# A four-layer graph network, software-pipelined over 64 samples: the order of steps on each engine chosen anew

## What is computed

```python
# layer 0: three projections, scores = (x W1)(x W2)^T
e = where(adj, leaky_relu(h1 @ h2.T), -big); out = relu(softmax(e) @ h3)
# layer 1: graph attention
h = x @ W; e = leaky_relu((h @ a1)[:, None] + (h @ a2)[None, :])
out = elu(softmax(where(adj, e, -big)) @ h)
# layer 2: mlp1 (256 to 512), attention without a mask on 512 features, mlp2 (512 to 256), attention with the mask
o = relu(x @ mlp1 + b1);  o = elu(gat(o, None, W_fc, a_fc)) + o
o = relu(o @ mlp2 + b2);  out = relu(elu(gat(o, adj, W_hand, a_hand)) + o)
# layer 3: attention of 4 heads with q, k, v, output projections and biases
out = softmax(mask(q @ k.T / 8)) @ v @ wo.T + bo
```

## Time and profile before

| | |
|---|---|
| three executions | 2769.3, 2783.66, 2788.16 us |
| span of the profiled execution | 2787.8 us |
| granted TensorE clock, mean over the span | 0.974 of full |
| PE busy | 2604.3 us, 93% of the span |
| DVE, ACT, POOL busy | 83%, 71%, 70% |

### The profile page before, as it was taken

How to read it: one execution, slowest core, us unless ns; L and a number is a source line. 1 busy time by engine, 2 the same in 40 slices (tenths; PEclk the granted TensorE clock), 3 DMA queues, 4 the chain that set the end, 5 groups by cost and what they waited for, 6 DMA issues and landing times.

```text
span 2787.8 us, 64765 instructions
## 1 busy us (share of the span) xinstructions
PE 2604.3 (93%) x21448; PEld 2453.2 (88%) x21448; DVE 2308.8 (83%) x6124; ACT 1985.1 (71%) x4801; POOL 1959.6 (70%) x2439
## 2 busy tenths in 40 slices
PE   4789999999999999999999999999999999999864
PEld 4689999999999999999999999999999999998763
DVE  2468888888888988888898898888889888888764
ACT  2357777777777777777777777777777777777642
POOL 1447777777777777777777787778777777776642
PEclk7799999999999999999999999999999999999986
DMA  3123434343443434344443434444343444333332
GB/s 129 49 59 116 136 116 135 116 134 113 126 130 118 133 114 137 112 124 131 123 128 118 131 116 129 123 130 121 118 136 116 127 120 132 120 118 118 95 95 87
DMA packets 317114, 329.67 MB, mean 118 GB/s; under 512 B 35312, under 2 KB 248688, under 8 KB 316784
## 3 DMA queue, kind: packets, MB, share of 16 engines
q1 hardware_dynamic: 316784, 325.54, 38.4%
HBM read 174.41 MB, written 150.99 MB: 117 GB/s over the span
## 4 chain that ended last, share of the span: by engine, by line
PE 34%; DVE 29%; POOL 13%; issue 10%; ACT 7%; DMA 5%; SPq 1%; POOLq 0%; DVEq 0%; ACTq 0%
PE ps L287 22%; POOL xn L1149 6%; DVE att L998 4%; PE ps L526 4%; DMA x0Tp<-in_xT 4%; DVE p L1102 3%; DVE att L993 3%; PE ps L297 3%; DVE p L1087 3%; POOL act L1159 3%; DVE ex L989 2%; DVE act L936 2%; ACT act L605 2%; POOL rstd L1144 2%; PE ps L303 2%
## 5 line engine op out<-in xcount | busy, mean ns | idle before, releaser
L1212 POOL TENSOR_TENSOR p<-p,rd 128x512 f32<-128x512 f32 x256 | 271.8, 1062 | 20.1
L1137 POOL TENSOR_TENSOR x0Tp_lo<-x0Tp,x0Tp_hi 128x512 fp32r<-128x512 f32 x64 | 82.6, 1291 | 288.0 <-ACT x0Tp_hi L542 288.0
L773 ACT ACTIVATE p<-p,nmx 128x256 f32<-128x256 f32 x512 | 256.0, 508 | 12.2 <-DVE nmx L1087 12.2
L1149 POOL TENSOR_SCALAR xn<-act,nmean,rstd 128x256 f32<-128x256 f32 x384 | 237.8, 629 | 23.6 <-POOL rstd L1144 22.5
L287 PE MATMUL ps<-h_lo,proT_hi 128*128 128x256 f32 x512 | 161.0, 314 | 62.9 <-POOL proT_lo L1137 61.9
L1087 DVE CUSTOM_DVE_ANT_0 p<-ps,mask 128x256 f32<-128x256 f32 x512 | 189.3, 417 | 31.2 <-PE ps L500 30.5
L542 ACT ACTIVATE h_hi<-ps 128x512 fp32r<-128x512 f32 x192 | 114.5, 596 | 123.2 <-PE ps L287 123.2
L1137 POOL TENSOR_TENSOR proT_lo<-sco,proT_hi 128x512 fp32r<-128x512 f32 x128 | 166.2, 1299 | 49.4 <-ACT proT_hi L542 49.3
L555 ACT ACTIVATE sco<-sco,nmax 128x256 f32<-128x256 f32 x384 | 190.8, 502 | 7.2 <-DVE nmax L859 6.5
L1159 POOL TENSOR_TENSOR act<-act,x 128x512 f32<-128x512 f32 x64 | 82.9, 1296 | 151.8 <-ACT act L605 151.8
L865 DVE STREAM_TRANSPOSE act<-sco 128x512 f32<-128x512 f32 x192 | 133.2, 694 | 57.2 <-ACT sco L555 56.3
(11 more groups left out here) (239 smaller groups left out, 12805.2 us busy)
## 6 DMA issues: line engine op xcount, KB each, us to landing
scratch<-p SPq DMA_DIRECT2D x128, 512.0 KB, 2.9
p4T<-scratch SPq DMA_DIRECT2D x512, 128.0 KB, 3.4
scratch_pro<-act SPq DMA_DIRECT2D x192, 256.0 KB, 2.4
sco<-scratch_pro SPq DMA_DIRECT2D x768, 64.0 KB, 2.4
x0Tp<-in_xT SPq DMA_DIRECT2D x64, 256.0 KB, 4.4
x<-in_x SPq DMA_DIRECT2D x64, 256.0 KB, 3.1
scratch_o<-sco SPq DMA_DIRECT2D x64, 256.0 KB, 2.0
o3r<-scratch_o SPq DMA_DIRECT2D x256, 64.0 KB, 2.1
```

Source lines behind the costliest of these rows:

```text
L773: ins = nc.scalar.activation(rows_, rows_, ACT.Exp, scale=-1.0, bias=nmx4[:, h, m:m + 1], accum_out=den4[:, h, m:m + 1])
L1137: return G.tensor_tensor(lo, whole, hi.bitcast(fp32), ALU.subtract)
L1149: ins = G.tensor_scalar(xn[:, m, :], y[:, m, :], nmean[i][:, m:m + 1], rstd[i][:, m:m + 1], ALU.add, ALU.mult)
L1212: G.tensor_tensor(rows_, rows_, rd4[:, h, :].unsqueeze(2).unsqueeze(3).broadcast_to([P, NT, QUADS, CT * QP]), ALU.mult).then_inc(S["p4n"], 1)
```

## The change

The five lists are replaced. The steps, their instructions, waits and buffers are the same. Most of the differences in the digits are a shift of a whole list or another place for the round's start, and change nothing. What is left, as moves within the cyclic sequence (all else keeps its place):

- PE: v4 goes ahead of x0; f2 goes from behind a4 to ahead of s0.
- ACT: t3 goes ahead of k2; r2 ahead of h0 and u1; p0 from behind f2 to behind q4; l0 ahead of k4; t1 ahead of b2; n2 ahead of x0; t0 from behind n2 to behind a1, so that o2 and the heads' exponentials come before it; p42 ahead of a1.
- DVE: i0 and i3 go behind s43; p42 goes from behind b1 to ahead of i2; a1 ahead of n2; g0 ahead of x42; r2 ahead of h0 and z3; f2 ahead of ag0, and both ahead of e1; o3 ahead of x1; t1 ahead of a4; x3 ahead of e0; h3 behind st4; t0 behind q4; e3 ahead of d2; ag4 ahead of t3; i1 between s40 and s41.
- POOL: n4 goes behind n3; k4 behind l0; v4 and m2 ahead of d40; t0 from ahead of d40 to between d42 and p42; t3 ahead of d43.
- SP: lt goes ahead of st, o1, o5, lx and o0; o0 goes behind i1 and o3; i3 and o40 ahead of i5.

```diff
 ORDERS = {
-    "sp": "o42:8 i40:8 i42:8 st:9 o1:3 o5:6 lx:1 o0:1 lt:0 i1:3 i0:1 o3:6 i5:6 i3:6 o40:7",
-    "pe": "x0:4 v4:9 b2:7 n2:6 s40:9 v2:7 w2:7 s42:9 a1:5 h1:4 g0:2 c2:6 a0:3 a3:8 f1:4 r2:6 h0:2 m3:7 s0:2 x1:5 a4:9 f2:6 x3:8 m2:5 y4:9 h3:7 q4:8 k4:8 f3:7 d2:6",
-    "ac": "t3:7 c2:5 g0:1 z2:6 a3:7 b3:7 a0:2 h0:1 u1:3 r2:5 m3:6 o3:6 s0:1 x1:4 p1:3 a4:8 x3:7 f2:5 p0:1 w2:5 h3:6 x2:5 m2:4 q4:7 u3:6 k4:7 l0:0 p3:6 b2:5 t1:3 x0:2 n2:4 t0:1 p40:7 o2:4 p41:7 y2:5 a1:3 p42:7 h1:2 p43:7 k2:5",
-    "dv": "i0:2 v2:6 s42:8 p41:8 s43:8 i2:6 b1:4 p42:8 n2:6 h1:3 p43:8 x40:8 a1:4 j2:6 c2:5 x42:8 g0:1 c3:7 z2:6 b3:7 a3:7 st1:4 r3:7 ag1:4 h0:1 z3:7 e1:3 st3:7 ag3:7 st0:2 r2:5 ag0:2 x1:4 a4:8 f2:5 e0:1 x3:7 t1:3 b2:5 y4:8 o3:6 t0:1 h3:6 st4:8 q4:7 d2:5 e3:6 k4:7 v4:7 t3:6 s40:7 s41:7 ag4:8 i3:6 x0:2 p40:7 i1:3",
-    "po": "l0:1 t1:4 t0:2 d40:8 p40:8 m2:5 d41:8 p41:8 d42:8 p42:8 d43:8 p43:8 t3:7 v4:9 y1:4 a0:2 n4:9 v1:4 n1:4 v3:7 n3:7 m3:6 v0:2 k4:7 n0:2 w2:5",
+    "sp": "o42:8 i40:8 i42:8 lt:0 st:9 o1:3 o5:6 lx:1 i1:3 o3:6 o0:1 i0:1 i3:6 o40:7 i5:6",
+    "pe": "f3:6 d2:5 v4:7 x0:2 b2:5 n2:4 s40:7 v2:5 w2:5 s42:7 a1:3 h1:2 c2:4 g0:0 a0:1 a3:6 f1:2 r2:4 h0:0 m3:5 f2:4 s0:0 x1:3 a4:7 x3:6 m2:3 y4:7 h3:5 q4:6 k4:6",
+    "ac": "k2:6 c2:5 g0:1 z2:6 a3:7 b3:7 a0:2 r2:5 u1:3 h0:1 m3:6 o3:6 s0:1 x1:4 p1:3 a4:8 x3:7 f2:5 w2:5 h3:6 x2:5 m2:4 q4:7 p0:1 u3:6 l0:0 k4:7 p3:6 t1:3 b2:5 n2:4 x0:2 o2:4 p40:7 p41:7 y2:5 p42:7 a1:3 t0:1 h1:2 p43:7 t3:6",
+    "dv": "st4:8 h3:6 q4:7 t0:1 e3:6 d2:5 k4:7 v4:7 ag4:8 t3:6 s40:7 i1:3 s41:7 x0:2 p40:7 v2:5 s42:7 p41:7 s43:7 i3:6 i0:1 p42:7 i2:5 b1:3 a1:3 n2:5 h1:2 p43:7 x40:7 j2:5 c2:4 g0:0 x42:7 c3:6 z2:5 b3:6 a3:6 st1:3 ag1:3 r3:6 r2:4 h0:0 z3:6 st3:6 ag3:6 st0:1 f2:4 ag0:1 e1:2 o3:5 x1:3 t1:2 a4:7 x3:6 e0:0 b2:4 y4:7",
+    "po": "v0:2 n0:2 w2:5 l0:0 k4:7 t1:3 v4:8 m2:4 d40:7 p40:7 d41:7 p41:7 d42:7 t0:1 p42:7 t3:6 d43:7 p43:7 y1:3 a0:1 v1:3 n1:3 v3:6 n3:6 n4:8 m3:5",
 }
```

## The result

| | before | after |
|---|---|---|
| median of the runs of this comparison | 2784.64 us (2769.3 to 2788.16) | 2674.89 us (2673.6 to 2674.92) |
| span of the profiled execution | 2787.8 us | 2671.8 us |
| a round, from one DVE v2 to the next, 700 to 2100 us | 40.54 us | 38.98 us |
| PE, DVE, ACT, POOL busy | 93, 83, 71, 70% | 95, 83, 74, 71% |

The ratio is 0.9622, with a 95% interval from 0.9594 to 0.965: 110 us less, where 50 were predicted.

The account below looks back on a forecast made before the run. PE was taken as the bound, with little left in the steady part. Waits of 41.6 us, 4 of hidden spacing and 4 to 5 in the drain made 50 us less: 2734 us from 2783.7, range 2714 to 2788.

Parts of the forecast that it names:

- 4 hidden: Steady part: 4 us of spacing lost at late inputs but left out of displayed idle, of some 6 possible.
- What bounds the kernel: Steady part: PE is the bound, busy 98% (688.57 of 700 us), with very little left to win.
- PE's wait before a3: PE's a3 waits for POOL's late t3; moving t3 earlier gains 29.6 us plus some 3 us not displayed.
- PE's wait before x1: PE's x1 waits for POOL's n1; n4 behind n3 and f2 ahead of x1 gain 12.0 us plus some 3 hidden.
- The usual spacing where a step changes its inputs: PE's borders between steps: matmuls follow by 0.21 us, between 0.2 and 0.3, once inputs are ready.
- What the DVE pays: DVE from v2 to c2: p42 waits 1.1 us, i2 shortens to 1.23 us; cover 0.2 us, cost nothing.
- DMA queue: SP's list: lt sooner is not felt by PE; o0 later costs nothing; i3 ahead of i5 helps the drain.
- i3 ahead of i5: 5 us, in the drain: SP's list in the drain: 1.5 us a round in three or four rounds, 5 us, between 0 and 20.
- All other moves: Remaining moves on all lists: cost nothing; if one is wrong, at most 0.4 to 0.8 us a round, 20 to 45 us.
- the first (p42 holds DVE): Rival, DVE's v2 to c2: p42 delays c2 and PE's r2, 40 us slower, 2824 us; chance 0.13.
- the second: Rival, ACT's t0 waits for o0's late data, t3 stays late; 2769 to 2784 us; chance 0.21 with the third.
- the third, the heads' DMAs: Rival, PE's a4: i42's data become late, 23 us given back, 2757 us; chance 0.21 together with the second.

Follow-up runs that it names:

- a_t3back: Changed kernel with POOL's t3 put back behind d43 and p43; 2796.18 us, ratio 1.0064 to the kernel before.
- a_n4back: Changed kernel with POOL's n4 put back ahead of v1 and n1; 2674.6 us, ratio 0.9632 to the kernel before.
- b_n4: Kernel before with only POOL's n4 moved behind n3; 2776.85 us, ratio 1.0005.
- b_p42: Kernel before with only p42 moved, ahead of a1 on ACT and ahead of i2 on DVE; 2799.9 us, ratio 1.0083.
- b_t3: Kernel before with only t3 moved, ahead of d43 on POOL and ahead of k2 on ACT; 2758.04 us, ratio 0.9919.
- b_t3_dve: Kernel before with t3 moved on POOL and ACT, p42 moved on ACT and DVE, and DVE's a1 ahead of n2; 2773.53 us, ratio 0.9974.
- a_ltback: Changed kernel with SP's lt put back behind st, o1, o5 and lx; 2671.98 us, ratio 0.9616 to the kernel before.
- b_t3_lt: Kernel before with t3 moved on POOL and ACT, and lt ahead of o0 in SP's list; 2746.37 us, ratio 0.9895.
- a_spold: Changed kernel with the old list of SP; 2977.01 us, ratio 1.0708 to the kernel before.
- b_spnew: Kernel before with the new list of SP alone; 3057.45 us, ratio 1.0998.
- a_dvold: Changed kernel with the old list of DVE; 3204.47 us, ratio 1.152 to the kernel before.
- a_peold: Changed kernel with the old list of PE; 2860.68 us, ratio 1.03 to the kernel before.

## Why the prediction was wrong

The sign and the mechanism that it named first were right; the size was less than half, and the time is outside the range. By parts of the span: the steady part was priced at 45.6 us (41.6 and 4 hidden) and gave 91; the fill was priced at nothing and gave 14; the drain at 4 to 5, and gave 11.

- *What bounds the kernel.* Right: PE, and its round cannot go below the spacing of 0.12 us. But the reading "very little left to win", from 98% busy, failed. A matmul is shown as 0.28 us long and the next starts 0.12 us after it, so up to 0.16 us of stall behind each is shown as busy. The kernel before had at least 1.56 us a round to give, of which 0.73 (41.6 / 57) was shown.
- *PE's wait before a3.* The mechanism was right: POOL's t3 was late, it is now 0.62 us early, and a_t3back brings the wait back. The term was mis-sized. From start to start the border went from 0.816 to 0.118 us, and the next matmul from 0.22 behind the first to 0.12: 0.80 us a round, where 32.6 us / 57 = 0.57 was priced.
- *PE's wait before x1.* Gone, by 0.37 + 0.06 = 0.43 us a round (from 0.496 to 0.125, and the second transpose from 0.166 to 0.108); priced at 15 / 57 = 0.26. The reason given for it was wrong: n4 behind n3 is neither needed (a_n4back) nor of use alone (b_n4). That f2 ahead of x1 covers it is the prediction's other reason; no run here takes that move alone.
- *Two borders that the prediction did not price.* Into r2 the distance fell from 0.200 to 0.044 us, and into m3 from 0.204 to 0.141, with 0.06 at the matmul behind. Neither shows up as a wait before. With these the four borders make 1.5 of the 1.56 us. "The usual spacing where a step changes its inputs", 0.2 to 0.3 us, was the step that failed: the prediction took it as a floor, and at these four borders 0.12 us or less was to be had in most rounds. At others (into a1 and a4) 0.2 us stays in both kernels.
- *What the DVE pays.* The layout was right within 0.6 us: p42 waits, i2 takes 1.20 us, c2 ends before r2 wants it (10.58 after v2; the prediction's 1412.8 is 11.2). "Cost nothing" was right for the changed kernel, where the move is even worth 12 us, and b_p42 shows the price where m2, t0 and t3 are not moved: 22 us. The rows on the shared port hold: POOL's `rd`, on 2 columns, started 0.16 us after i2, was shown as 1.10 us long and ended with it. The Trainium skill's page "SBUF — State Buffer", section "SBUF: two separate sides", calls this port an exclusive lock that the first comer keeps to its end; b_p42 agrees, since i2 falls from 2.04 to 1.21 us, in 21 of 35 rounds, by nothing but a later start. j2 was priced at 1.2 us and takes 1.43.
- *What takes the place of the wait.* The prediction asked what is late next and named the heads' DMAs. What was late next in b_t3 was DVE's x42, held by p43 behind t3 on POOL, and PE before m3 behind that: the prediction counted p43's delay for nobody. b_t3 and b_t3_dve show it. In the change g0 stands in the hole, a move that the prediction left without a price.
- *DMA queue.* "i3 ahead of i5: 5 us, in the drain" was wrong in place and size: 32 us, in the steady part, because ACT's t3 asks sooner. That lt is nothing that PE feels holds for its place against st, o1, o5 and lx (a_ltback), not for lt ahead of o0, which gives much of the fill's gain (b_t3_lt); and o0's place and t0's and p0's on ACT go together: the new list of SP alone costs 10%, the old one in the changed kernel 7%.
- *All other moves.* The bound of 0.4 to 0.8 us a round was far too low for a list as a whole: undoing PE's alone costs 186 us against the changed kernel, DVE's alone 530.
- *Fill and drain.* Nothing was priced in the fill; 14 us were won there. The move with the largest share on record is lt ahead of o0: it wins 8.5 us in b_t3_lt, where PE's wait for the second sample's `x0Tp_lo` falls to 4.6 us, and with SP's old list in the changed kernel (a_spold), where that wait is 8.5 us again, nothing is left of the 14. It isn't enough by itself: b_spnew has the short wait (4.8 us) and gains nothing by the 1000th matmul. Part stays open: b_p42 and b_n4 also gain 4 to 5 us there, without a move that would explain it. The drain's 11 us need t3 (a_t3back gains nothing there), and t3 alone brings 6 of them (b_t3).

The rivals: the first (p42 holds DVE) came true only where p42 is moved alone; the second was real in b_spnew and is avoided by t0's new place; the third, the heads' DMAs, does not show (no wait of PE before a4 in the steady part).

How the parts add up: t3, p42 and i3 undone singly cost 121, 12 and 32 us, more than the 110 us that all of the change brought. Alone in the kernel before they bring 20, -22 and (with t3) nothing. A round has several chains of nearly equal length that end at PE, and a cure is worth only the distance to the next. No set of moves tried in the kernel before brought more than 36 us. Which smallest set gives the whole gain stays open: the changed kernel without the new list of SP, of PE or of DVE is slower than the kernel before, but that shows only that the lists fit each other, not which of their moves the gain needs. No run takes PE's f2 and c2, DVE's g0, r2 and f2, or the group of o0, t0 and p0 by itself. No kernel tried was faster than the changed one by more than its measurement is uncertain (a_ltback and a_n4back equal it).

## What to carry to other kernels

When the order of steps is a set of in-order queues, price a change of order from the whole of the new layout and not as a sum of cured waits: a move cures one late input and delays what it was put ahead of, so for each move ask who waits for the step that was passed, and whether something else fills that hole. Measure PE's loss from one matmul's start to the next, against the spacing inside a step, and border by border between two kernels, since some borders keep a wider spacing: displayed idle of some tenths of a microsecond was here less than half of what there was to win. And look at a DMA that is read by a step moved forward first: its place in the queue becomes critical at that moment, and not before.

## What was not expected of the hardware

- A late input costs PE more than the shown idle time: 0.28 us each in a_t3back (1.86 against 1.58 us a round). Some 0.16 us of it is the time by which a shown matmul (0.28) outlasts the spacing (0.12), and 0.10 that the matmul behind the late one starts 0.22 us after it instead of 0.12.
- Which DVE instructions meet POOL on the port was read off only for i2. n2 (L989), with a single input, seems to as well: 0.68 us in b_t3_dve, 0.87 in the changed kernel, where it starts 0.33 us before POOL's `gT_lo` ends, and 1.45 in the kernel before. That `gT_lo` took 1.48 us instead of 1.30; DVE's b1 (L941, also a single input) had started 0.10 us before it. DVE's block transpose (L1102, 1.22 us) ran beside POOL's `proT_lo` (1.30 us) with neither of them longer.
- The kernels that leave PE waiting longest also got less clock. From 1400 to 2100 us PE is busy 88% in a_dvold, 92% in a_spold and 95% in a_peold, and the granted clock averaged 0.95, 0.95 and 0.99 instead of 1.00, so a part of the time was spent at the lower of the two levels (1.2 and 2.4 GHz). In a_spold the distance into s40 grew by 3.5 us over the changed kernel, and the matmuls behind it, 0.12 us apart in the changed kernel, start up to 0.20 us apart; of the 5.0 us that its round is longer, some 1.5 lie there (an estimate: 5.05 less the 3.5 of that border). a_t3back, busy 96% with waits of at most 2.0 us, kept 1.00. The rows of a_dvold and a_spold:

```profile
1400.00:2100.00 700.00, 617.75 (x4901) 581.18 (x4902) 516.12 (x1390) 449.68 (x1105) 427.08 (x554) 0.95 0.35 105
1400.00:2100.00 700.00, 644.63 (x5294) 618.87 (x5293) 542.62 (x1510) 486.11 (x1192) 473.24 (x602) 0.95 0.37 114
```
